# Two attention stages of a transformer kernel: where the input is transposed, and when the output projection runs

## The reference, cut to what matters

```python
# layer 0
q = (layernorm(x) @ Wq).reshape(B, N1, H, hd).transpose(0, 2, 1, 3)
attn = softmax(einsum('bhqd,bhkd->bhqk', q, k) * scale)        # 77 context tokens
o = einsum('bhqk,bhkd->bhqd', attn, v)...reshape(B, N1, C1)
x = x + (o @ Wproj + bproj)
x = x + (gelu(layernorm(x) @ W1 + b1) @ W2 + b2)
# layer 1
h = layernorm(x);  x = x + mha(h, h, sa_wq, ...)               # 512 keys
h = layernorm(x);  x = x + mha(h, context, ca_wq, ...)         # 77 keys
h = layernorm(x);  x = x + gelu(h @ w1.T + b1) @ w2.T + b2
```

## Time and profile before

| what | us |
|---|---|
| median of three runs (3521.05 to 3522.68) | 3521.89 |
| the profiled execution, its own time | 3518.35 |
| its span from first to last instruction | 3516.6 |
| PE busy | 3189.1 (91%) |
| DVE busy | 1833.4 (52%) |
| ACT busy | 1587.1 (45%) |
| POOL busy | 1329.1 (38%) |
| mean granted clock of PE | 0.959 of full |

### The profile page before, as it was taken

One profiled execution on the slowest core, in us unless ns is written; L12 is line 12 of the kernel. 1 busy time (PEld: TensorE's weight loads), 2 busy tenths in 40 slices (PEclk: granted clock), 3 DMA queues, 4 the chain that ended last, 5 costly groups with the idle time before them and its releaser, 6 DMA issues. The chain is left out here.

```text
span 3516.6 us, 41925 instructions
## 1 busy us (share of the span) xinstructions
PE 3189.1 (91%) x14480; PEld 2523.2 (72%) x14480; DVE 1833.4 (52%) x2848; ACT 1587.1 (45%) x2980; POOL 1329.1 (38%) x1355
## 2 busy tenths in 40 slices
PE   6599997999999968999999999848999799999999
PEld 5477775888888845666766676636777588888887
DVE  4577773333322225777777777747777542222221
ACT  2365553322222224666666666625666342222222
POOL 0344441333333323666656666634444211111110
PEclk8799998999999978999999999978999899999999
DMA  4322213211111122343334333331222230000111
GB/s 141 111 63 72 74 54 122 81 48 48 49 48 48 49 80 80 94 118 103 106 109 114 107 95 107 95 92 54 79 73 63 98 101 32 32 33 32 32 34 36
DMA packets 215045, 264.33 MB, mean 75 GB/s; under 512 B 78459, under 2 KB 100579, under 8 KB 214835
## 3 DMA queue, kind: packets, MB, share of 16 engines
q1 hardware_dynamic: 214835, 261.66, 25.0%
HBM read 125.12 MB, written 60.42 MB: 53 GB/s over the span
## 5 line engine op out<-in xcount | busy, mean ns | idle before, releaser
L1065 DVE TENSOR_REDUCE L1sa_nmax<-L1sa_s 128x2 f32<-128x1024 f32 x256 | 310.6, 1213 | 209.2 <-PE L1sa_s L884 209.2
L1157 POOL TENSOR_TENSOR L1sa_El<-L1sa_E,L1sa_Eh 128x1024 fp32r<-128x1024 f32 x128 | 320.4, 2503 | 148.5 <-ACT L1sa_Eh L972 142.3
L468 DVE TENSOR_TENSOR L1ff_gl<-L1ff_gf,L1ff_gh 128x512 fp32r<-128x512 f32 x128 | 95.4, 745 | 472.9 <-ACT L1ff_gh L428 472.9
L468 DVE TENSOR_TENSOR L0ff_gl<-L0ff_gf,L0ff_gh 128x512 fp32r<-128x512 f32 x128 | 97.5, 762 | 439.1 <-ACT L0ff_gh L428 439.1
L414 ACT ACTIVATE L0ff_gf<-L0ff_f,cols 128x512 f32<-128x512 f32 x128 | 88.3, 690 | 450.1 <-PE L0ff_f L94 450.1
L414 ACT ACTIVATE L1ff_gf<-L1ff_f,cols 128x512 f32<-128x512 f32 x128 | 88.3, 690 | 449.7 <-PE L1ff_f L94 449.7
L981 ACT ACTIVATE L1sa_E<-L1sa_st 128x1024 f32<-128x1024 f32 x256 | 260.3, 1017 | 45.9 <-PE L1sa_st L896 45.9
L92 PE MATMUL L0ff_f<-L0ff_hTh,L0ff_Wh 128*128 128x512 f32 x512 | 203.0, 396 | 5.8 <-POOL L0ff_hTl L235 5.8
L92 PE MATMUL L1ff_f<-L1ff_hTh,L1ff_Wh 128*128 128x512 f32 x512 | 202.9, 396 | 5.7 <-POOL L1ff_hTl L235 5.7
L972 ACT ACTIVATE L1sa_Eh<-L1sa_E 128x1024 fp32r<-128x1024 f32 x192 | 200.6, 1045 | 0.2
L94 PE MATMUL L0ff_f<-L0ff_hTl,L0ff_Wh 128*128 128x512 f32 x512 | 200.2, 391 | 0.0
(11 more groups left out here) (282 smaller groups left out, 8569.6 us busy)
## 6 DMA issues: line engine op xcount, KB each, us to landing
L1sa_OLN<-L1sa_osb SPq DMA_DIRECT2D x128, 192.0 KB, 2.7
L0ff_xs<-x SPq DMA_DIRECT2D x64, 256.0 KB, 2.9
L1sa_stack_q<-L1sa_parts_q SPq DMA_DIRECT2D x128, 128.0 KB, 2.6
L1sa_stack_k<-L1sa_parts_k SPq DMA_DIRECT2D x128, 128.0 KB, 2.6
L1ff_xs<-x SPq DMA_DIRECT2D x64, 256.0 KB, 3.4
L0ca_xs<-in_x SPq DMA_DIRECT2D x32, 256.0 KB, 3.1
L0ca_stage<-in_x SPq DMA_DIRECT2D x32, 256.0 KB, 2.8
x<-L0ca_stage SPq DMA_DIRECT2D x32, 256.0 KB, 2.0
```

The lines of the kernel that those rows point to most:

```text
L468: nc.vector.tensor_tensor(gl[:, j % 2, :], gf[:, j % 2, :], f32(gh[:, j % 2, :]), ALU.subtract)\
L1065: nc.vector.reduce_max(nmax[:, h % 2, 2 * (n % 2):2 * (n % 2) + 2], s_bank[:, :, :], AX.X, negate=True)\
L1157: nc.gpsimd.tensor_tensor(El[:, n % 2, :], E[:, n % 3, :], f32(Eh[:, n % 2, :]), ALU.subtract)\
```

## The change

Transpositions are no longer units. In self attention `h_transposed(b + 1, t)` runs in the halves 22, 26, 28 and 30 (`SA_T_HALVES`), right after that half's product with V, and writes to the bank of the unit that comes next, while the unit at hand is half way through in the other bank. In cross attention the transpositions run in the halves 3, 4, 5 and 6 (`T_HALVES`) and use the banks `t0` and `t1`, in turn with the transpositions of the softmax weights. The projections' quarters now fill the halves alone: 64 quarters in 64 halves, and 32 in 24. ACT and DVE get the evacuations of the transpositions as calls of their own (`h_hi`, `h_lo`; `whole`, `hi`, and `lo` on POOL). In self attention ACT's `m_copy` moves ahead of the evacuations, and DVE adds the output projection (`finish("O")`) at the head of a step instead of at its end. Before the first batch ACT and DVE evacuate the transpositions between the weights instead of after them. On SP the loads, stores and residual loads of self attention move to other steps.

```diff
-SA_ORDER = [("q", 0, 2), ("k", 0, 2), ("O", -1, 0), ("O", -1, 1), ("q", 0, 3), ("k", 0, 3), ("T", 1, 0), ("T", 1, 1), ("O", -1, 2), ("O", -1, 3), ("T", 1, 2), ("T", 1, 3), ("q", 1, 0), ...
+SA_ORDER = [("q", 0, 2), ("k", 0, 2), ("O", -1, 0), ("q", 0, 3), ("k", 0, 3), ("O", -1, 1), ("O", -1, 2), ("O", -1, 3),
+            ("q", 1, 0), ...
+SA_T_HALVES = (22, 26, 28, 30)
...
+        T_unit = {(0, t): t % 2 for t in range(TT)}
+        for b in range(1, B):
+            for t, half in enumerate(SA_T_HALVES):
+                kind, ahead, i, _ = halves[half][-1]
+                n = b - 1 + ahead
+                T_unit[b, t] = (no[kind, n, i] if n >= 0 else no["k", b - 1, 3] + t % 2) + 1
...
-                    if s in (13, 14) and b + 1 < B:
-                        load(b + 1, s - 11)
-                    if s in (18, 19) and b + 2 < B:
-                        load(b + 2, s - 18)
-                    if b > 0 and s in (7, 9, 16, 18):
-                        store(b - 1, (7, 9, 16, 18).index(s))
-                    if b > 0 and s in (9, 11):
-                        load_residual(b - 1, 2 + (9, 11).index(s))
+                    if s in (12, 14) and b + 1 < B:
+                        load(b + 1, 2 + (s - 12) // 2)
+                    if s in (15, 17) and b + 2 < B:
+                        load(b + 2, (s - 15) // 2)
+                    if b > 0 and s in (7, 13, 15, 17):
+                        store(b - 1, (7, 13, 15, 17).index(s))
+                    if b > 0 and s in (8, 14):
+                        load_residual(b - 1, 2 + (s - 8) // 6)
...
+            def h_transposed(b, t):
+                u = T_unit[b, t]
+                pe.wait_ge(hs_full[t % 2].sem, hs_full[t % 2].no((b * TT + t) // 2))
+                earlier = [other for other in T_before[u] if other < (b, t)]
+                if earlier:
+                    pe.wait_ge(e_hl.sem, e_hl.at(*earlier[-1]))
+                elif u >= 2:
+                    evacuated(u - 2)
...
-            weights_hi(0, QK_CHUNKS)
+            for t in range(2):
+                h_hi(0, t)
+            weights_hi(0, 2)
+            for t in range(2, TT):
+                h_hi(0, t)
+            weights_hi(2, QK_CHUNKS)
...
-CA_ORDER = ([("Q", 0, 3)] + [("T", 1, c) for c in range(KT)]
-            + [("O", -1, 0), ("Q", 1, 0), ("O", -1, 1), ("Q", 1, 1), ("O", -1, 2), ("O", -1, 3), ("Q", 1, 2)])
+CA_ORDER = [("Q", 0, 3), ("O", -1, 0), ("O", -1, 1), ("Q", 1, 0), ("O", -1, 2), ("Q", 1, 1), ("O", -1, 3), ("Q", 1, 2)]
+T_HALVES = (3, 4, 5, 6)
...
+            def turn_bank(kind, b, i):
+                at = turn[kind, b, i]
+                if at >= 2:
+                    before, n, j = turns[at - 2]
+                    if before == "T":
+                        pe.wait_ge(x.e_hf.sem, x.e_hf.at(n, j))
+                    else:
+                        pe.wait_ge(e_pl.sem, e_pl.at(n, j))
+                return t_bank[at % 2]
```

More of the change, by code:

```diff
@@ L844, in piece @@
                 bank = pj[u % 2]
-                if c == 0 and u >= 2:
+                if c == 0:
                     bank_free(u)
-                if kind == "T":
-                    pe.wait_ge(hs_full[i % 2].sem, hs_full[i % 2].no((b * TT + i) // 2))
-                    for j in range(KT):
-                        last = nc.tensor.transpose(bank[:, j * P:(j + 1) * P], hs[:, i % 2, j * P:(j + 1) * P],
-                                                   cst.ident[:, :])
-                    last.then_inc(e_tr.sem, e_tr.unit)
-                    return
                 if kind in "qk":
@@ L936, in _ @@
             cst.wait_ident(pe)
+            for t in range(TT):
+                h_transposed(0, t)
             for kind, i in SA_FIRST:
@@ L1048, in _ @@
                         exp(n + LEAD_T)
+                    if n % 2 == 0 and 0 <= n + 6 < PAIRS:
+                        m_copy((n + 6) // 2)
                     if n >= 0:
@@ L1052, in _ @@
                                 evacuate(kind, b_of, i)
-                    if n % 2 == 0 and 0 <= n + 6 < PAIRS:
-                        m_copy((n + 6) // 2)
+                        for t, half in enumerate(SA_T_HALVES):
+                            if half // 2 + half % 2 == n % STEPS and b + 1 < B:
+                                h_hi(b + 1, t)
             o_out(HEADS - 1)
@@ L1500, in cross_attention @@
         no = {u: i for i, u in enumerate(units)}
+        turns = [("T", 0, c) for c in range(KT)]
+        for b in range(B):
+            for half in range(HALVES):
+                if half % 2 == 0:
+                    turns.append(("P", b, half // 2))
+                if half in T_HALVES and exists(b + 1):
+                    turns.append(("T", b + 1, T_HALVES.index(half)))
+        turn = {u: i for i, u in enumerate(turns)}
         def tile_at(half):
@@ L1698, in _ @@
                         PV(b - 1, CA_STEPS - 1)
+                    if half in T_HALVES and exists(b + 1):
+                        T(b + 1, T_HALVES.index(half))
             PV(B - 1, CA_STEPS - 1)
@@ L1762, in _ @@
             weights_hi(0, WQ)
+            for c in range(KT):
+                whole(0, c)
             for u in CA_FIRST:
@@ L1776, in _ @@
                         p_hi(b, half // 2)
+                    if half - 1 in T_HALVES and exists(b + 1):
+                        whole(b + 1, T_HALVES.index(half - 1))
                     for u in evacs[b * HALVES + half]:
@@ L1867, in _ @@
                 normalise(0, t)
+            for c in range(KT):
+                hi(0, c)
             for u in CA_FIRST:
@@ L1894, in _ @@
                         p_lo(b, half // 2)
+                    if half - 1 in T_HALVES and exists(b + 1):
+                        hi(b + 1, T_HALVES.index(half - 1))
                     for u in evacs[b * HALVES + half]:
```

126 lines of the change are left out of this document (71 added, 55 removed).

## The result

The changed kernel takes 3471.53 us (median of 4 runs, 3465.93 to 3473.08), the kernel before 3521.83 us (4 runs, 3521.05 to 3522.68): ratio 0.9854, 95% interval 0.9837 to 0.9871. The forecast was 3468 us. The profiled execution took 3465.93 us, with a span of 3464.1 us. The sum in the prediction gave 3464.3 us for it.

The account below looks back on a forecast made before the run. PE, busy 91%, bounds the kernel. Self attention 14.7, its start 3.7 and cross attentions 35.6 us make 54 off 3518.35: 3464.3, plus 3.5 for the median: 3468 us. Own range 3455 to 3481; 8 in 10, 3430 to 3499.

Parts of the forecast that it names:

- The late load: Self attention, last transposition: waits 3.7 us every batch for its tokens in `hs`, loaded behind `line_up` and eight stack DMAs.
- The estimate of 0.2 us less: Load into `hs`: by the skill's fit 2.6 us instead of 2.8, new wait 0.2 us shorter; the forecast kept the row.
- the load not being late: Rival: SP reaches the load some 4 us sooner, so waits and low clock go too, 3431 us; chance 0.12.
- The waits that go, together 6.0 us: Self attention, per batch: PE's waits for `rx` 2.6, `parts_k` 1.5, `oTl` 1.4 and `hTl` 0.5 us go.
- The first output projection starts in step 4: Self attention: two V products and four score instructions, 1.4 us, come ahead of it, as much as it waited for `oTl`.
- I take nothing for it: Self attention: DVE's additions at a step's head delay its maximum 0.7 us at most, next scores 3.3 us later; cost nothing.
- changes nothing in the sum: Self attention: low clock behind the old wait loses 1.7 us; the new 3.7 us wait brings the same loss.
- 3.16 - 0.4 = 2.8 us: Cross attention, six batches each: waits of 1.77 and 1.39 us go, 0.4 us of new waits come.
- The start: Start of self attention: transpositions interleaved with weight conversion, first query projection from 1316.5 instead of 1320.25, 3.7 us gained.
- The change moves the waits and no more: Rival: PE's waits go, but the softmax's chain of scores, maximum, exponential ends last instead, 3522 us; chance 0.05.
- More waits in cross attention: Rival: 2 us per batch come back at the turns of `t0` and `t1`, 28 us less gain, 3496 us; chance 0.14.
- the turns bind: Rival: cross attention, halves 4 to 6, every filling of `t0` and `t1` waits out an evacuation, 3567 us; chance 0.06.

Follow-up runs that it names:

- the early load: Changed kernel with SP's loads of `h` in steps 12 and 14 put ahead of the stacks of their step: 3430.31 us, ratio 0.9736.

## Why the prediction was right in total and wrong in its parts

- **The late load: right.** Wait forecast 3.7 us, measured 3.63 to 3.75 in six batches and 4.46 in the first. In the first batch the third transposition waits 1.38 us too, and before the change this batch waited 3.30 us: 4.46 + 1.38 - 3.30 = 2.5 us more, as forecast. The estimate of 0.2 us less is from a section on DMAs that POOL issues, while SP issues these; the row's 2.8 us gave the measured wait. Forecast for the load not being late: 3431 us, measured with the early load 3430.3 (5.4 us a batch forecast, 5.75 measured).
- **"The waits that go, together 6.0 us": failed.** The steps that failed are two. "The first output projection starts in step 4", with `oTl` at nothing: it still waits 0.91 us. And of DVE "I take nothing for it": the scores wait 1.17 us more for the maximum, though not by the additions of which that was said. The waits of one batch before (2.61, 0.44, 0.55, 0.66, 0.46, 1.35, 1.58) make 7.65 us, after (3.73, 1.72, 0.64, 0.45, 0.36, 0.91) 7.81. Forecast was 7.65 - 2.3 = 5.35. Of the missing 2.46 us (rounded), 1.17 are the maximum, 0.91 `oTl` and 0.36 one more wait for E, whose cause is open. The cause of the first is shown: DVE's `oTl` stands behind POOL's `El` for longer, and without that 9 to 14 us come back. The second has the same cause by the rows (2.57 us for 0.68), and it too went when POOL's `El` was moved. The prediction added up DVE's durations as those of a free engine; it has no term for what POOL does beside it.
- **The clock "changes nothing in the sum": a little off.** The low clock cost some 2 us a batch after and 1.7 by the estimate before. Where the wait ended the clock had been low for a while already, which the rows below show.
- **"3.16 - 0.4 = 2.8 us" in cross attention: mis-sized.** It is 3.6: the 0.4 us of new waits did not come, and PE's busy time fell by 0.45 us, for which the sum had no term. Over six batches and two stages that is 10 us. Of the other 6 us, 1.6 are the batch of `L1ca` at mean clock 0.97 before. The first batches gained 1.1 and 0.1 us where 1 was forecast, and the rest lies behind the start of the last batch, from where to the next stage it is 107.6 us before and 103.1 after in `L0ca`, 109.7 and 101.4 in `L1ca`; that is not taken apart. The sum held PE's busy time fixed, and 11 of the 51.6 us are less of it.
- **The start: 3.7 forecast, 3.0 to 3.2 measured.** The third transposition waits 4.45 us for its input, and on DVE its evacuation stands ahead of the last weights, for which the projection then waits 4.03 us.
- **Rivals.** "The change moves the waits and no more" was given 0.05; for the self attention alone its outcome is what happened, but its mechanism is the smaller part: in place of the 6.0 us came 3.7 us of the late load, as forecast, and some 2.5 us of the chain on DVE, behind POOL. "More waits in cross attention" and "the turns bind" did not come.

## What to carry to other kernels

A wait that is removed leaves two things behind: what was hidden by it (here a load behind eight DMA issues in one queue), and a new relative position of engines that share something (here DVE and POOL). Check both for the same place before you book the gain; the first is read from the queue of issues, the second from operations whose duration varies in the profile. Book the parts of a sum by stage, so that the result can be held against them: a right total proves none of them. And an edit is measured on the kernel where its wait was seen, since on the next one (here with the early load) it may not exist.

## What was not expected of the hardware

One DVE operation of 128 x 512 (`oTl`) takes 0.68 us alone and up to 2.6 us in the changed kernel, when it starts inside POOL's `El`; in all 28 such places there, and in all 21 of the kernel before, it ended 0.54 to 0.56 us after POOL's. The other way round, with the early load, POOL's `El` took 2.86 instead of 2.40 us when it started inside DVE's `oTl`.

The clock fell while PE still stood waiting for the load, as the stretches around 1518.08 us in the changed kernel show:

```profile
1514.00:1516.00 2.00, 0.45 (x2) 0.00 (x0) 0.55 (x1) 0.00 (x0) 1.72 (x3) 1.00 0.68 174
1516.00:1518.00 2.00, 0.00 (x0) 0.00 (x0) 0.00 (x0) 0.00 (x0) 0.00 (x0) 0.68 0.75 244
1518.00:1520.00 2.00, 1.92 (x7) 1.73 (x8) 0.14 (x1) 0.60 (x1) 0.00 (x0) 0.50 0.83 166
1520.00:1522.00 2.00, 2.00 (x7) 1.41 (x6) 1.24 (x2) 0.63 (x2) 0.53 (x1) 0.50 0.32 124
1522.00:1524.00 2.00, 2.00 (x7) 1.60 (x6) 0.93 (x1) 1.81 (x2) 0.01 (x1) 0.62 0.33 93
```

PE was idle from 1514.45 and at 1.2 GHz until about 1523.5. At the same wait four batches later (1997.08, 3.70 us) the low clock covered less of PE's work: 0.50 and 0.65 in the two stretches from 1998 on, 1.00 from 2002. Waits of 1.3 and 1.7 us at this place left it at 1.00. The length of the wait alone does not decide: in the middle of `L1ca` before, PE waits 1.83 us for `qTl` six times, and behind the first of them (2434.55) the clock is 0.66 and 0.50 in the two stretches from 2435 us on, while the next batches stay at a mean of 1.00.
